# Weight units before the first value tile, value tiles over three attention steps, and one weight product by tile, in a graph-network kernel

## The reference, cut to what matters

```
h = relu(layernorm(x)); x = x + L0(h)     # attention over heads and nodes, then a feed-forward part
h = relu(layernorm(x)); x = x + L1(h)     # linear, then twice: sum over edges, two products, batch norm
h = relu(layernorm(x)); x = x + L2(h)     # H = X @ W, normalised sum over edges, leaky relu ("gcn")
h = relu(layernorm(x)); x = x + L3(h)     # two relational layers

# L0:  q, k, v = x@Wq+bq, x@Wk+bk, x@Wv+bv        (8 heads of 64)
#      scores = q.k / 8, -1e9 where there is no edge
#      attn = softmax(scores, axis=heads); out = attn.v @ Wo + bo
# L3:  w = einsum('rb,bio->rio', att, basis)       (2 relations, 30 bases of 512 x 512, in 2 layers)
#      msg = sigmoid(x_j @ gate[r]) * x_j @ w[r]; agg + x @ root + bias
```

## Time and profile before

| what | value |
|---|---|
| median of 3 runs | 457.75 us (457.6 to 458.14) |
| the profiled execution: its own time, its span | 456.62 us, 454.8 us |
| DVE, ACT, POOL busy | 346.3 (76%), 243.7 (54%), 42.9 (9%) us |
| chain that ended last | PE 70%, DVE 12%, DMA 8%, issue 8% |
| moved by DMA | 99.22 MB, mean 218 GB/s |
| granted TensorE clock | 1.00 over the span |

### The profile page before, as it was taken

How to read it: one execution, slowest core, us unless ns; L and a number is a source line. 1 busy time by engine, 2 the same in 40 slices (tenths; PEclk the granted TensorE clock), 3 DMA queues, 4 the chain that set the end, 5 groups by cost and what they waited for, 6 DMA issues and landing times.

```text
span 454.8 us, 6200 instructions
## 1 busy us (share of the span) xinstructions
PE 438.6 (96%) x2226; PEld 274.3 (60%) x2226; DVE 346.3 (76%) x736; ACT 243.7 (54%) x428; POOL 42.9 (9%) x59
## 2 busy tenths in 40 slices
PE   8999999899997899999999999999998999999997
PEld 3334554443432346768776866677465788888885
DVE  5999996899999968688779657675759695866212
ACT  5999994676897617543345436544534623511210
POOL 3240000024223011000010000010000000000000
PEclk9999999999999999999999999999999999999999
DMA  7997347426699859978099766777973550000002
GB/s 254 415 398 176 110 174 308 179 93 219 235 380 353 295 206 332 409 272 345 11 372 404 295 246 251 275 252 267 375 199 115 225 186 1 1 0 2 0 3 92
DMA packets 18090, 99.22 MB, mean 218 GB/s; under 512 B 2959, under 2 KB 3599, under 8 KB 7567
## 3 DMA queue, kind: packets, MB, share of 16 engines
q1 hardware_dynamic: 13191, 72.72, 43.4%
q0 software_dynamic: 4000, 25.18, 15.1%
q10 hardware_dynamic: 864, 0.86, 0.6%
HBM read 93.50 MB, written 5.25 MB: 217 GB/s over the span
## 4 chain that ended last, share of the span: by engine, by line
PE 70%; DVE 12%; DMA 8%; issue 8%; ACT 1%; POOL 0%; DVEq 0%; POOLq 0%
PE bank L1371 15%; PE sbank L1703 10%; PE bank L1716 6%; PE sbank L1357 6%; PE sbank L1427 6%; PE bank L1608 5%; DMA bring<-in_basis 4%; PE bank L1688 4%; PE sbank L1567 3%; PE bank L1450 3%; DMA wring<-in_weights 3%; PE bank L1357 3%; PE bank L1513 2%; PE sbank L1337 2%; PE sbank L1490 2%
## 5 line engine op out<-in xcount | busy, mean ns | idle before, releaser
L839 DVE TENSOR_SCALAR cnt<-iota_row,edge_f 128x512 bf16<-128x512 f16 x132 | 41.4, 350 | 0.4 <-PE sbank L1427 0.4
L1357 PE MATMUL sbank<-bring,attw 120*32 120x512 f32 x336 | 41.0, 599 | 0.1
L1427 PE MATMUL sbank<-cnt,adjT 128*128 128x512 bf16 x132 | 30.6, 380 | 0.3
L466 ACT ACTIVATE stat<-stat,eps 128x1 f32<-128x1 f32 x32 | 9.4, 294 | 39.3 <-DVE stat L858 39.3
L576 ACT ACTIVATE adjT<-distance,edge_w,edge_f 128x128 bf16<-128x128 bf16 x61 | 29.2, 479 | 1.4 <-PE sbank L1427 1.4
L1281 DVE SCALAR_TENSOR_TENSOR y_lo<-sbank,gate,y_hi 128x512 fp32r<-128x512 f32 x16 | 11.8, 750 | 22.6 <-ACT y_hi L765 22.5
L497 ACT ACTIVATE s<-bank,colsb 128x512 f32<-128x512 f32 x24 | 16.4, 687 | 21.8 <-PE bank L1371 21.8
L1427 PEld LDWEIGHTS sbank<-cnt,adjT 128*128 128x128 bf16 x132 | 12.3, 98 | 21.7 <-DVE cnt L839 6.4
L529 ACT ACTIVATE distance<-iota_row,edge_f 128x128 bf16<-128x128 f16 x61 | 24.3, 400 | 1.8 <-DVE edge_f L905 0.4
L1371 PE MATMUL bank<-hT_hi,w_hi 128*128 128x512 f32 x64 | 25.3, 395 | 0.0
L1371 PE MATMUL bank<-hT_hi,w_lo 128*128 128x512 f32 x64 | 24.9, 390 | 0.0
(11 more groups left out here) (250 smaller groups left out, 1092.5 us busy)
## 6 DMA issues: line engine op xcount, KB each, us to landing
bring<-in_basis SPq DMA_DIRECT2D x59, 1024.0 KB, 9.8
wring<-in_weights POOLq DMA_DIRECT2D x8, 1024.0 KB, 10.0
landing<-in_weights POOLq DMA_DIRECT2D x4, 1024.0 KB, 5.1
w_scratch<-stage SPq DMA_DIRECT2D x16, 256.0 KB
hT<-in_weights POOLq DMA_DIRECT2D x4, 1024.0 KB, 9.1
qkw<-w_scratch POOLq DMA_DIRECT2D x2, 2048.0 KB, 7.9
rring<-in_rows POOLq DMA_DIRECT2D x12, 256.0 KB, 8.5
wring<-in_basis SPq DMA_DIRECT2D x2, 1024.0 KB, 12.9
```

The source lines that it names most:

```text
L839: dve.tensor_scalar(hot_s[:, n % HOT, :], iota[:, :], src_f[:, n:n + 1], None, ALU.is_equal).then_inc(sem("hot_ready"), 1)
L1357: mm = pe.matmul(unit_bank(b)[32 * j:32 * j + 32, :], attw[0:KB, u // UNITS, g, :], unit_place(u)[0:KB, j, :], start=(g == 0), stop=(g == ...
L1427: pe.matmul(bank[7][:, :], hot_d[:, n % HOT, :], hot_s[:, n % HOT, :], start=(n == 0), stop=(n == ECH - 1)).then_inc(sem("hot_used"), 1)
```

## The change

Four units (8 to 11) stand where V0 stood, before the mask of step 0. V0 takes the place of V1, and V1, V2 and V3 stand in steps 0, 1 and 2. `STEP_UNITS` is 1, 0, 1 in the first three steps in place of 1, 2, 3, so that the number of units up to the end of attention is as before. All value tiles use bank 3, and batches 2 and 3 both use bank 2: PE waits before unit 12, the first of batch 3, until batch 2 has been copied (`stage_ready` 3). ACT copies batch 2 in step 0, behind `exps(1)`. DVE takes V1 to V3 behind the first sum of steps 1 to 3. POOL loads the row g2 after four scalings in place of two. In the gcn part the product runs tile by tile (`BY_TILE`), and `root1` is loaded when the product `c2_1` is done in place of when `x5` is.

```diff
-STEP_UNITS = (1, 2, 3, 3, 3, 3, 3, 0)
-ATTENTION_BATCHES = (EARLY_UNITS + sum(STEP_UNITS)) // BATCH + 1
+STEP_UNITS = (1, 0, 1, 3, 3, 3, 3, 0)
+ATTENTION_BATCHES = (EARLY_UNITS + BATCH + sum(STEP_UNITS)) // BATCH + 1
...
-             "root1": ("x5", C), "root2": ("c2_1_psum", C)}
+             "root1": ("c2_1_psum", C), "root2": ("c2_1_psum", C)}
...
-            return bank[(2 if b < ATTENTION_BATCHES else 6) + b % 2]
+            if b < ATTENTION_BATCHES:
+                return bank[2 if b < 4 else 3 - b % 2]
+            return bank[6 + b % 2]
...
-                scale_heads(0)
-                scale_heads(1)
-                load_row("g2", "v")
-                for it in range(2, 2 * C - 1):
+                for it in range(2 * C - 1):
                     scale_heads(it)
+                    if it == C - 1:
+                        load_row("g2", "v")
...
-                    stage_units(STEP_UNITS[it])
+                    stage_units(STEP_UNITS[it] + (0 if it else BATCH))
...
                 take_v(0)
-                take_v(1)
...
-                    after(step(dve.tensor_tensor(four_sums, sc[:, 0:4, :], sc[:, 4:8, :], ALU.add)))
+                    n = step(dve.tensor_tensor(four_sums, sc[:, 0:4, :], sc[:, 4:8, :], ALU.add))
+                    if 1 <= it < C:
+                        take_v(it)
+                    after(n)
...
-                    if it < 2:
-                        take_v(2 + it)
...
-                        if g == 0 and b == EARLY_UNITS // BATCH:
-                            pe.wait_ge(sem("v"), 1)
-                        elif g == 0 and b == EARLY_UNITS // BATCH + 1:
+                        if g == 0 and b == EARLY_UNITS // BATCH + 1:
+                            pe.wait_ge(sem("stage_ready"), b)
+                        elif g == 0 and b == EARLY_UNITS // BATCH + 2:
                             pe.wait_ge(sem("v"), C)
...
                 products(0, 0)
-                qkv_tile(2 * C)
+                units(BATCH)
                 pe.wait_ge(sem("no_edge"), 1)
                 exclude(0, 0, "scores_psum")
...
-                qkv_tile(2 * C + 1)
+                qkv_tile(2 * C)
...
-                    if it < 2:
-                        qkv_tile(2 * C + 2 + it)
+                    if it < C - 1:
+                        qkv_tile(2 * C + 1 + it)
                     units(STEP_UNITS[it])
...
-                parts_stage("gcn", hT_parts, "agg2", "gcn_psum", t_major=False)
+                parts_stage("gcn", hT_parts, "agg2", "gcn_psum", order=BY_TILE, t_major=False)
```

More of the change, by code:

```diff
@@ L293, in wait_unit @@
             pe.wait_ge(sem(f"basis{r % BATCH}_loaded"), 16 * (r // BATCH + 1))
-        def v_bank(c):
-            return 3 if c else 2
         def place_of(h):
@@ L874, in take_v @@
                     dve.wait_ge(sem("v_psum"), c + 1)
-                    dve.tensor_tensor(vr[:, c, :], bank[v_bank(c)][:, :], row("bv"), ALU.add).then_inc(sem("v"), 1)
+                    dve.tensor_tensor(vr[:, c, :], bank[3][:, :], row("bv"), ALU.add).then_inc(sem("v"), 1)
                 for c in range(C):
@@ L1438, in qkv_tile @@
                     elif which:
-                        pe.wait_ge(*((sem("v"), c) if c >= 2 else (sem("k"), C)))
-                    at = v_bank(c) if which == 2 else c
+                        pe.wait_ge(*((sem("v"), c) if c else (sem("k"), C)))
+                    at = 3 if which == 2 else c
                     if which == 1:
```

## The result

| | before | after |
|---|---|---|
| median of 4 runs | 457.94 us (457.60 to 459.25) | 464.38 us (464.11 to 466.04) |
| ratio after / before | | 1.0144, 95% interval 1.0115 to 1.0172 |
| profiled execution: own time, span | 456.62, 454.8 us | 464.50, 462.7 us |
| granted TensorE clock over the span | 1.00 | 0.987 |

What follows compares the result with a forecast made beforehand. PE, busy 438.6 of 454.8 us, was taken as the bound. Attention's +5.5 (1.75 from unit 11, 3.7 from unit 12's stall) less 1.0 in the gcn part gave +4.5, on a median of 457.75: 462.2, range 458.6 to 464.5.

Steps and rivals of the forecast that it cites:

- Part 1: Units before the mask: PE waits 1.9 us for unit 11's load, making DVE's chain and V0 1.75 us later.
- Part 2: Before unit 12 PE stands 4.35 us for ACT's copy of batch 2; step 2's scores and unit 14 come 5.5 later.
- the clock falls in the stall: Rival, 15%: behind unit 12's idle wait 17 matmuls run slow, 1.8 us on top, 464.0 in all.
- Part 3: Steps 5 and 6: earlier basis loads gain nothing, as ring and queue are full; 3.8 us of waits stay.
- Part 4: Gcn part: early root1 and tile order gain 2.5 us, waits at units 59 and 60 cost 1.5; net gain 1.0.
- the new order: Gcn product by tile: tile 0 ready at 339.6, not 342.3, which carries 1.6 of the 3.6 us DVE gains.
- `root1` split ends before 343: Sign for the gcn part: DVE's split of root1, which ended at 344.3, ends before 343; the sum had 340.7.
- The faster one: Rival, 8%: early loads count, the three basis waits in attention vanish, and the total is 456.4.
- no stall at unit 12: Rival, 7%: batch 2 is copied before PE comes, only part 1 is left of attention, 458.5.
- The root1 load hurts nobody: Rival, 10%: root1's early load delays neither unit 59 nor 60; 5.5 - 2.5, 460.7.
- The sum: Whole kernel: attention 5.5 less gcn 1.0 gives +4.5 us, 461.1 for the profiled execution, 462.2 for the median.

Runs made afterwards that it cites:

- e3: The changed kernel with unit 12 moved behind the scores of step 2 (STEP_UNITS 0, 1, 1): 459.94 us, ratio 1.0049 to the kernel before.
- e5: The changed kernel with filler matmuls on zeros in both waits, 18 ahead of unit 12 and 8 between units 10 and 11: 461.78 us, ratio 1.0072.
- e4: The changed kernel with 18 filler matmuls on zeros ahead of unit 12, the stall kept: 461.79 us, ratio 1.0089 to the kernel before.
- e8: The changed kernel with unit 11 behind the tally product and STEP_UNITS 0, 1, 2, 3, 3, 3, 2, 0: 462.82 us, ratio 1.0106.
- e9: The kernel before with only the gcn product run tile by tile, root1 still loaded behind x5: 457.55 us, ratio 0.9986.
- e10: The kernel before with only root1's load moved ahead, behind c2_1, product in the old order: 455.25 us, ratio 0.9940.
- e1: The kernel before with the gcn part alone, root1 loaded behind c2_1 and product by tile: 456.29 us, ratio 0.9969.
- e11: The kernel before with the gcn product by tile and root1's load issued when unit 59 has been read: 455.87 us, ratio 0.9961.
- e2: The changed kernel with the gcn part put back as before, so the attention part alone: 465.54 us, ratio 1.0187 to the kernel before.
- e6: The changed kernel with three units ahead of the mask and unit 11 behind the tally product: 462.50 us, ratio 1.0097.
- e12: e11 with four filler matmuls on zeros ahead of each of units 22, 24 and 25: 455.34 us, ratio 0.9926 to the kernel before.
- e7: The changed kernel with unit 11 behind the tally product and STEP_UNITS 0, 1, 1, so e3 and e6 together: 457.49 us, ratio 0.9990.

## Why the prediction went wrong, step by step

**Part 1, the wait for unit 11: right, its consequence short.** 2.04 us for 1.9, the mask at 81.97 for 81.8. But `find_max` began at 85.79, 3.35 behind the 82.44 of the earlier trace rows, and not 1.75 behind. Most of the other 1.6 is the clock. From the mask's start to V0 PE took 85.60 - 81.97 = 3.63 us in after and 84.35 - 82.10 = 2.25 in e3, the same matmuls at the 2.4 GHz level.

**Part 2, the stall of unit 12: right, its consequence short.** 4.25 us for 4.35, with the copy behind `exps(1)` as its end. That the lists up to unit 14 take as long as before held too: in e5 it is 23.50 us from the scores of step 2 for 23.44, and unit 14 stands at 124.38 for 124.2.

**The step that failed** is the rival "the clock falls in the stall". It had 15% and a price of 1.8 us, and the forecast's own sum had the clock at 1.00 throughout, so its term for the lower clock was nothing, at both waits. It was the case at both. It cost 2.3 behind the stall (e4 against after) and 1.5 ahead of unit 12, behind unit 11's wait (e5 against after; about 0.1 of it is a shorter wait): 3.8 together, and 5.5 + 3.8 = 9.3 for the 9.45 seen. The chance was too low because of the argument against it, that the longest wait in the trace of before, 1.5 us, was followed by fast matmuls. That says nothing about a wait of 4.35, almost three times as long, which no row of before resembles. The price was too low because I took it from 17 matmuls at the start, though the matmuls behind the stall are the path itself and all of them slow down: a unit by 0.87, the scores and masks of the first four heads by 1.4, a little of the next. And unit 11's wait wasn't considered for the clock at all. The rule of the Trainium skill cited there, "TensorE: Matmul & The Clock Gate", section on the HAM clock gate, that an idle array falls to half its clock, agrees with the 0.50 of 100 to 105 us; for the longer wait it deserved more weight than the forecast gave it.

**Part 3, the early loads give nothing: right.** 3.55 us of waits in steps 5 and 6 for 3.8, no DMA traffic from 100 to 115 us with the ring full. The lateness of 9.45 at unit 14 is still 9.4 at the units before the gcn product. e8 shows it from the other side: moved units move the waits and don't shorten them.

**Part 4, the gcn part: the sum nearly right, its parts not.** -1.6 for -1.0. The early `root1` was to bring 2.5 and cost 1.5; it brings 2.6 and costs 0.9 to 1.0. That the new order carries 1.6 of it is wrong (e9, e10): DVE's lead ends at the product's end on PE in either order, so an earlier first tile is only a wait of DVE for the turned tile, 1.77 us, in place of one for the product, 1.83. The waits for relu7 are 0.36 and 0.25, for the 0.5 of the forecast. The sign "`root1` split ends before 343" was given in the time of the kernel before, without the lateness of attention: it ends at 350.3 in after, which less 9.4 is 340.9, for 340.7 in the sum.

**The rivals.** The faster one (early loads count) and "no stall at unit 12" are refuted by the rows above. "The root1 load hurts nobody" is refuted: PE waits 1.48 and 0.66 at units 59 and 60, and unit 61 is 0.9 to 1.0 late in e1 and e10 and not in e11.

**The sum again.** By the profiles: attention 9.45, the gcn part -1.6, together 7.85 for the 7.88 of the two profiled executions. By the medians it is 6.4. Nearly all of the difference lies in before: its profiled execution took 456.62, 1.3 under its median of 457.94, while that of after took 464.50, 0.1 over its own. On the profiled executions the forecast was 3.4 short: 3.95 at unit 14, less 0.6 for the gcn part. That the median of after, 464.38, lies inside a range that reached to 464.5 is thus partly luck. The mean clock doesn't order the four executions either: one of 0.996 took 464.11 and the one of 0.987 took 464.50. So the 3.8 us are shown for the profiled execution, and what the clock cost in the others is not. The forecast with both clock terms would have been 466.0, 1.6 over the median.

## What to carry to other kernels

A wait of PE on the path costs its own length and, behind it, the slower matmuls until the clock is back: here 4.25 + 2.3. So where a change adds a wait of some us to a busy PE, look for what of that length the trace has, and if it has nothing, count the lower clock in, not out; filler matmuls into a free bank give it back at no cost while the wait lasts. Before a unit of work is moved ahead in one list, find the copy in another engine's in-order list that frees its buffer; here moving unit 12 by one step saved 4.4 us. And before a late weight is loaded earlier, look which loads it is put in front of: here that cost 0.9 to 1.0 of the 2.6 it brought, and nothing once those loads were through.

## What the runs showed of the hardware

- The TensorE clock fell to the 1.2 GHz level behind every wait of 3.6 to 4.3 us that was profiled (after, e2, e6, e8) and behind none where matmuls on zeros filled it (e4, e5). Behind e8's wait of 3.08 us, at the end of attention, it read 1.00. Behind a wait of about 2 us it fell in some executions (after 2.04, e4 1.82) and not in others (e2 1.82, e3 2.00). Behind two shorter waits in a row, with a unit between them, it fell in the profiles of e1 (0.49 and 1.31 us) and e11 (1.24 and 1.30) and not in that of before (1.03 and 1.29).
- These falls are most of the spread between executions of e11: 454.6 to 459.0 us at clocks of 0.991 to 1.000, 454.6 to 455.4 for the five at 0.999 or more, and 454.9 to 455.6 in e12, where fillers stand in those waits. In e7 executions at 1.000 spread over 2.7 us, which the clock doesn't explain.
- The wait that the trace names can be the wrong one of two that end within 0.1 us (e8).
